# Moving the bias, the context and three steps of the router inside the second attention's batches

## The reference

```
x = x + attn_a(layernorm(x))     # linear attention with a causal mask, 16 heads of 8
x = x + ffn(layernorm(x))        # router: 2 of 16 experts per token, with a capacity
x = x + attn_b(layernorm(x))     # per head: the 6 queries whose largest score is highest
x = x + ffn(layernorm(x))        # the same experts and the same router again
```

```
scores = einsum('bhqd,bhkd->bhqk', Q, K) * scale
top_u  = top_k(scores.max(axis=-1), 6)[1]          # the 6 queries of each head
attn   = softmax(Q[top_u] @ K^T * scale)
ctx    = attn @ V                                   # put back at top_u, zeros elsewhere
out    = padded_ctx @ wo.T + bo
...
probs  = softmax(xf @ router_w);  w, idx = top_k(probs, 2)
oh     = one_hot(idx, 16)
rank   = cumsum(oh, axis=0) - oh                    # place of a token in its expert's queue
keep   = rank < capacity;  slot, dispatch, wbuf follow from rank and idx
```

## Time and profile before

| | us |
|---|---|
| median of 3 runs | 1438.34 |
| lowest and highest run | 1431.31, 1448.30 |
| profiled execution, its own time | 1437.23 |
| its span in the trace | 1435.5 |
| PE busy | 1261.4 (88%) |
| DVE busy | 1064.1 (74%) |
| POOL busy | 835.8 (58%) |
| ACT busy | 758.6 (53%) |

### The profile page before, as it was taken

One profiled execution on the slowest core, in us unless ns is written; L12 is line 12 of the kernel. 1 busy time (PEld: TensorE's weight loads), 2 busy tenths in 40 slices (PEclk: granted clock), 3 DMA queues, 4 the chain that ended last, 5 costly groups with the idle time before them and its releaser, 6 DMA issues.

```text
span 1435.5 us, 28623 instructions
## 1 busy us (share of the span) xinstructions
PE 1261.4 (88%) x8534; PEld 796.5 (55%) x8534; DVE 1064.1 (74%) x4590; ACT 758.6 (53%) x1901; POOL 835.8 (58%) x1246
## 2 busy tenths in 40 slices
PE   3999998996998999999999999999999999999200
PEld 1565665555898955555444444544444469889100
DVE  2899999895664468888899888888987765656322
ACT  2444443442755767766666666656666456656000
POOL 3237776677625124556676766657673445457775
PEclk9999998998999989999999999979998799999655
DMA  6745502011546410001000000020000125467522
GB/s 170 256 155 179 190 31 82 28 41 60 186 153 205 155 53 15 16 16 31 24 25 27 27 27 28 25 85 24 27 27 12 38 67 162 144 207 208 154 75 71
DMA packets 119769, 125.82 MB, mean 88 GB/s; under 512 B 15552, under 2 KB 109888, under 8 KB 119616
## 3 DMA queue, kind: packets, MB, share of 16 engines
q1 hardware_dynamic: 103232, 90.42, 19.8%
q0 software_dynamic: 16384, 33.59, 8.2%
HBM read 50.15 MB, written 73.79 MB: 86 GB/s over the span
## 4 chain that ended last, share of the span: by engine, by line
PE 67%; DVE 15%; issue 5%; POOL 5%; ACT 2%; DMA 2%; SPq 1%; ACTq 0%; DVEq 0%; POOLq 0%
PE pair L1865 25%; PE pair L1791 9%; POOL vmyg L549 5%; PE pair L1653 5%; DVE pT L1387 4%; PE pair L1802 4%; PE bank L1677 3%; DVE pT L1112 3%; PE pair L1780 2%; PE bank L1598 2%; PE pair L1642 2%; PE bank L1592 1%; DVE xs L1304 1%; PE bank L1904 1%; PE bank L1884 1%
## 5 line engine op out<-in xcount | busy, mean ns | idle before, releaser
L1865 PE MATMUL pair<-kT,apart 32*128 32x512 f32 x2048 | 474.9, 701 | 13.7 <-DVE smax L1387 12.2
L910 ACT ACTIVATE pT<-pair 128x256 f32<-128x256 f32 x1024 | 331.4, 395 | 216.8 <-PE pair L1865 213.7
L1387 DVE CUSTOM_DVE_ANT_0 pT<-pair,pT 128x256 f32<-128x256 f32 x1024 | 385.0, 416 | 64.3 <-ACT pT L910 58.1
L1865 PEld LDWEIGHTS pair<-kT,apart 32*128 32x128 f32 x2048 | 201.2, 199 | 139.5 <-DVE smax L1387 84.4
L549 POOL DMA_INDIRECT vmyg<-ybufA,slg x128 | 123.8, 967 | 106.7 <-DVE smax L1387 58.8
L1791 PE MATMUL pair<-xeT,unit_w 128*128 128x256 f32 x768 | 185.1, 385 | 0.0
L549 POOL DMA_INDIRECT vmyg<-ybufB,slg x128 | 122.9, 960 | 78.9 <-DVE smax L1387 40.3
L1112 DVE TENSOR_TENSOR pT<-pair,causal 128x512 f32<-128x512 f32 x256 | 159.5, 681 | 11.8 <-PE pair L1653 11.4
L1279 DVE TENSOR_TENSOR hid<-sg,pair 128x512 f32<-128x512 f32 x96 | 65.9, 686 | 132.5 <-ACT sg L836 132.3
L494 POOL DMA_INDIRECT dispB<-xnf,sli x128 | 129.6, 1012 | 53.8 <-issue 34.9
L494 POOL DMA_INDIRECT dispA<-xnf,sli x128 | 129.3, 1010 | 49.6 <-issue 31.5
(11 more groups left out here) (230 smaller groups left out, 1969.4 us busy)
## 6 DMA issues: line engine op xcount, KB each, us to landing
dispB<-zeros SPq DMA_DIRECT2D x16, 1408.0 KB
apart<-dispA SPq DMA_DIRECT2D x96, 128.0 KB
ybufA<-ye SPq DMA_DIRECT2D x48, 256.0 KB, 2.3
apart<-dispB SPq DMA_DIRECT2D x96, 128.0 KB
ybufB<-ye SPq DMA_DIRECT2D x48, 256.0 KB, 2.7
dispA<-zeros SPq DMA_DIRECT2D x33, 128.0 KB
xs<-in_x SPq DMA_DIRECT2D x16, 256.0 KB, 3.2
out<-xs SPq DMA_DIRECT2D x16, 256.0 KB, 2.5
```

What stands on the lines that cost most here:

```text
L910: act.activation(rel[n % RING][:, q, :], pair[n % RING][:, q, HALF:SEQ], ACT.Relu).then_inc(s["relu_done"], 1)
L1387: dve.tensor_tensor_reduce(out=rel[n % RING][:, q, :], in0=pair[n % RING][:, q, 0:HALF], in1=rel[n % RING][:, q, :], scale=1.0, scalar=LOW ...
L1865: pe.matmul(pair[n % RING][:, q, :], apart[h][at, j, t * P:(t + 1) * P], kTs[h][at, HALF:], start=True, stop=True).then_inc(s["bsc_done"], 1)
```

## The change

In the second attention, and only there, steps change their place:

- POOL: `add_bias` moves from between the third and fourth tiles' sends to behind the second tile's, ahead of the norm of batch b + 2.
- DVE: `context` goes from pair 25 to 26 (behind `route_max` and pair 26), `route_best` and `route_which` one pair later (27, 28), `context_out` to 29, `route_choice` to 30. `route_hot` and `route_counts` leave the batch: they now come in pairs 1 and 2 of the next one, and `route_ranks` comes in pair 4 in place of 3. `selected_max` goes from 17 to 18, the first half of `add_first` from 18 to 17.
- PE: `ranks` behind pair 4's scores in place of pair 3's, `turn_exp` at 22 in place of 21, `context_out` at 30 in place of 29. ACT: `selected_exp` at 20, `turned_exp` at 22.
- Behind the last batch, `route_hot` and `route_counts` open the experts' first group on DVE.

No instruction with work in it is added or removed. The diff, cut where it repeats this list:

```diff
@@ POOL, body
                 send_tile(20, 1)
+                add_bias(b, b + B, b_bo)
                 if fetch_:
                     norm_scale(att_call(b + 2), TB)
                     normed(b + 2, b + 2 + B, xnb[(x + 2) % 4], "att", 0, att_call(b + 2))
                 send_tile(26, 2)
-                add_bias(b, b + B, b_bo)
                 send_tile(29, 3)
@@ ACT, body
-                    if last and n == 19:
+                    if last and n == 20:
                         selected_exp(b - 1)
...
-                    if last and n == 21:
+                    if last and n == 22:
                         turned_exp(b - 1)
@@ DVE, body
-                    if b >= 3 and n == 3:
+                    if b >= 3 and n == 1:
+                        route_hot(b - 3 + B)
+                    if b >= 3 and n == 2:
+                        route_counts(b - 3 + B)
+                    if b >= 3 and n == 4:
                         route_ranks(b - 3 + B, bank[0])
...
-                    if last and n == 17:
+                    if fetch and n == 17:
+                        add_first(b + 2, h, (0, 1))
+                    if last and n == 18:
                         selected_max(b - 1)
-                    if fetch and n in (18, 19):
-                        add_first(b + 2, h, ((0, 1), (2, 3))[n - 18])
+                    if fetch and n == 19:
+                        add_first(b + 2, h, (2, 3))
...
-                    if last and n == 25:
-                        context(b - 1)
                     if before and n == 25:
                         route_max(b - 2 + B, bank[0])
-                    if before and n == 26:
+                    if last and n == 26:
+                        context(b - 1)
+                    if before and n == 27:
                         route_best(b - 2 + B)
-                    if before and n == 27:
+                    if before and n == 28:
                         route_which(b - 2 + B)
-                    if last and n == 28:
+                    if last and n == 29:
                         context_out(b - 1)
-                    if before and n == 28:
+                    if before and n == 30:
                         route_choice(b - 2 + B)
-                    if before and n == 29:
-                        route_hot(b - 2 + B)
-                    if before and n == 30:
-                        route_counts(b - 2 + B)
@@ DVE, pieces(0) of the experts behind the last batch
                 if g == 0:
+                    route_hot(b - 2 + B)
+                    route_counts(b - 2 + B)
                     residual(b - 1)
@@ PE, body
-                    if b >= 3 and n == 3:
+                    if b >= 3 and n == 4:
                         ...
                         ranks(b - 3 + B, bank[0])
...
-                    if last and n == 21:
+                    if last and n == 22:
                         turn_exp(b - 1)
...
-                    if last and n == 29:
+                    if last and n == 30:
                         context_out(b - 1)
```

## The result

The change makes the kernel slower: 1470.88 us (median of four runs, 1467.19 to 1487.63) against 1442.79 us of the kernel before on the same chip, a ratio of 1.0205 [1.0162, 1.0248]. The forecast was 1434 us, no change, with a range from 1416 to 1455. The profiled execution took 1469.24 us (span 1467.5), against 1437.23 (1435.5): 32.0 us of span more.

A forecast was written before the change was run, and what follows sets the result against it. Middles taken as bound by PE, variation in the boundaries. From 1437.2 us: boundaries -16.0, middles -5.9, experts +0.7 give 1416.0 at full clock; low clock +18.2 gives 1434 us, range 1416 to 1455.

The forecast's parts named there:

- cast out of the path: Boundaries, ahead of pair 0: the long DVE cast goes in eleven batches; its 1.48 us of excess cost 1.2 us each.
- ranks late: Front of each batch from the fourth: comparisons, counts and one pair more precede the ranks on DVE, 1.2 us per boundary.
- lefts: Last five batches: two more steps in the counts now lie ahead of the ranks, 5 x 0.53 = 2.7 us.
- sums in pair 17: First half of `add_first` on DVE, moved to pair 17: nothing in the sum, a collision with POOL's norm only a rival.
- start of the experts and the rest: Experts' start: the ranks' products wait 1.8 us, pair 31 ends about 1.1 us earlier, net +0.7 us.
- low clock, by difference: Boundaries and middles: low clock taken out in the full-clock sum, then 18.2 us put back for new stretches.
- The bias and the cast: POOL's 1.29 us bias fits 2.38 us of idle behind the second tile's sends; the DVE cast falls to 0.15 us.
- Context and selected maximum: Pairs 26 and 18: both DVE waits for PE go, costed at nothing; 0.1 us off pair 0's start, range 0 to 0.4.
- The ranks' wait: PE ahead of the transpose: waits about 1.2 us per batch, making the full-clock boundary 12.9 us, as with the long cast.
- The step that failed: Low clock after PE's new wait: 1.0 us at each of 13 boundaries and some four longer at 1.3 each, +18.2 us.
- its slow rival: From pair 5's transpose into the middle: low clock lasts longer, 3.5 us a batch, 13 times, 1461 us; chance 0.16.
- the sums meet the norm: Pair 17: DVE's sums are held by POOL's norm, at most 0.55 us x 11 = 6 us, 1440 us; chance 0.08.

The follow-up runs named there:

- c4: Changed kernel with the ranks back in pair 3 on DVE and PE, comparisons and counts left in pairs 1 and 2: 1456.54 us, 1.0094 of before.
- c1: The kernel before, unchanged, run for its trace on another chip: 1438.13 us (one run).
- d2: Changed kernel with the ranks in pair 3 and the first choice's sums back behind pairs 18 and 19: 1443.65 us, 1.0031 of before.
- e2: Changed kernel with the router part undone (comparisons and counts in pairs 29 and 30, ranks in pair 3): 1530.19 us, 0.9874 of before.
- d3: Kernel before with only the bias moved and the context, its scaling and the selected maximum one pair later: 1429.85 us, 0.9934 of before.
- d4: Kernel before with the bias alone in its new place: 1427.84 us, 0.9919 of before.
- g3: Same kernel as g1 plus an unread DVE maximum of 0.68 us in pair 1 of each batch from the fourth: 1441.17 us, 1.0004 of before.
- d1: Changed kernel with the turn of the maxima, its copy on ACT and DVE's top-place steps one pair later: 1475.21 us, 1.026 of before.
- g1: Kernel before with bias and context moved, nothing of the router or sums (as d3), as a base: 1425.26 us, 0.9878 of before.
- f1: Kernel of d3 plus an unread DVE maximum in pair 1 of each batch from the fourth: 0.987 of before, which takes 1566.51 us there.

## Why the prediction was wrong

Its own terms against the two traces, the forecast's rounded sum being 1434 (15 boundaries +7.5 us, 15 middles +24.8, the rest -0.3):

| term | forecast, us | measured, us | from |
|---|---|---|---|
| cast out of the path, 11 batches | -12.9 | -13.0 | 13.44 - 12.26 (one of the 11 casts took only 0.77 us) |
| ranks late, 13 batches | +15.6 | +19.1 | 13.73 - 12.26 |
| lefts | +2.7 | +2.3 | four waits of 1.24 to 1.66 in place of 0.79 |
| sums in pair 17, 13 batches | 0 | +9.1 | 27.07 - 26.37 in c4 and c1; the sums are 0.80 of it (d2: 26.27), less 0.10 for the later context and selected maximum |
| start of the experts and the rest | +0.7 | -0.3 | |
| low clock, by difference | -9.1 | +14.8 | |
| sum | -3.0 | +32.0 | |

The table takes each of the 13 batches alike. At 983.29 us, where DVE also makes the experts' tables, PE waited 2.85 us for the ranks; what that is over the others is in the last difference too. The forecast's low clock is what its sum held without naming it: it took 27.3 us out (its -21.9 for boundaries and middles less the first three terms) and put 18.2 back.

- **The bias and the cast: right**, in time and mechanism. The casts at 0.14 us include those beside a send (672.43, beside one from 672.28 to 673.25). By the rule of the Trainium skill weighed in the prediction ("SBUF — State Buffer", section "Who interferes with whom") a send would hold them all. The traces agree in part. In all of them with the bias moved, a cast that began up to 0.52 us into a send took 0.14 us, one that began 0.56 to 0.75 us into it ended with it and took 0.22 to 0.40. So in e2, where the send ends at 739.72:

```profile
738.75 0.97 POOL L494 DMA_INDIRECT dispA<-xnf,sli  x1 [0.31 <-issue]
```

```profile
739.34 0.37 DVE L1049 CAST topf<-top8i 128x8 f32<-128x8 uint32 x1
```

- **Context and selected maximum: right.** Both waits went, and d3 and d4 are equal within their intervals.
- **The ranks' wait: right in place and nearly in size.** PE's own idle ahead of the transpose is 0.79 us, not 1.2, since the rest of the delay already shows in the buffers; the boundary grew by 1.47 where 1.2 were forecast. The boundary at full clock is 0.3 us longer than one with the long cast, not "as long as" it.
- **The step that failed: "After the change it starts later, so I take the upper one, 1.0, at each of 13 boundaries, and some four longer ones".** It let the new stretches replace the old ones at a lower price in all: 18.2 us in place of the 27.3 it took out. They did come later, as it said, but they were longer (127 us at 1.2 GHz over the windows, in place of 91) and lay where PE is the bound: PEclk is 0.89 to 0.95 in twelve of the 15 middles, where nine of before had 1.00. What was priced at 18.2 us measures 18.2 + 23.9 = 42 by difference; the 23.9 us are the larger part of the 35 us of the miss. The prediction had this as its slow rival, at 3.5 us a batch, and gave it 0.16; 42 / 13 = 3.2 us a batch is close to that, and past the 2.8 at which the rival says slower. What spoke for it was the chain of waits, which I read near 905 us only: where the low clock doesn't cover it, it lies on DVE from pair 0 to the ranks, so that DVE work put there can hold PE in every pair, through the buffers, and not only at the transpose. In g3 such work brought, on average, more low clock with it.
- **The rival "the sums meet the norm" came true too**, at more than its price: 0.80 us in each of 13 middles, 10 us, not 6. The half microsecond I counted as cover was DVE's wait for the selected scores; by the order of the work (no run separates it) it is none, since the selected maximum now stands behind the sums, and PE's turn of the exponentials hangs on it. The Trainium skill ("SBUF — State Buffer", section "Who interferes with whom") has such an instruction contend with a GpSimd one that reads SBUF; the trace agrees, 1.47 us against 0.61 for the two. I costed a collision I had both a row and a rule for at nothing in the sum.

What stays open: why TensorE's clock falls where it does. It isn't PE's wait at the transpose, since d1 has no such wait and as much low clock as the changed kernel, and in g1, with no wait above 0.1 us in most batches, nine of the 15 boundaries still have a low stretch. The averages above show only that it lasts longer, the more DVE work stands ahead of the ranks. That this is because PE works with gaps there is argued, not shown. The 15 us of the table are by difference; the granted clock, with 35 us more at 1.2 GHz over the windows, allows up to 18.

## What to carry to other kernels

Before moving work on an engine, read the chain of waits through the place where it is put, not only the place it leaves: if the chain is on that engine there, the work costs nearly its full length (0.6 of 0.68 us here), and more where the engine behind it then runs at a lower clock. Off that stretch it was cheaper but not free (0.3 us). Waits of an engine that is off the chain (here DVE's for the context) were worth nothing, and the cheap cure, POOL's bias out of the way of a small cast, was worth 0.8% by itself while the rest of the change lost nearly 3%. A known collision belongs in the sum.

## What the runs showed of the hardware

- A 128 x 8 cast on DVE took 0.14 us when it began early in an indirect send of POOL, lasted to the send's end (0.22 to 0.40 us) when it began 0.56 to 0.75 us into it, and took 1.6 to 1.85 us when a POOL tensor addition stood directly behind the send.
- Two sums on DVE, each of two tensors in SBUF, took 1.47 us beside POOL's norm, 0.61 behind it.
- Stretches at 1.2 GHz began ahead of a transpose at which PE had no wait over 0.1 us (d1, from 765.5 us on).
- The same program took 1442 us on one chip and 1567 on another. The traces of close variants put the larger part outside the second attention: 874 us there in f1, 785 in d3.
